# Value matmuls of two key steps side by side, and the division and the split of the maxima on GpSimd, in a four-layer cross-attention and expert network

## The chip, the cores and the metric

The kernel runs on 1 core of a Trainium2 chip (trn2). The metric is the device time of one execution in microseconds (us). Three executions of the kernel before gave 4185.41, 4183.80 and 4180.53 us, with a median of 4183.8 us. The engines are named as in the profile: PE (TensorE matmuls), PEld (TensorE weight loads), DVE (VectorE), ACT (ScalarE), POOL (GpSimd), SP (SyncE, which here only issues DMAs).

## The reference

A sequence x of 2048 tokens with 256 features goes through four layers. Each layer adds a cross-attention over a context of 1601 rows with 192 features, and then a mixture of experts. The change touches the attention alone. Cut to what matters:

```python
def xattn(x, y):                       # x: 2048 x 256 (normalized), y: 1601 x 192
    q, k, v = heads(x @ Wq + bq), heads(y @ Wk + bk), heads(y @ Wv + bv)
    att = softmax(q @ k.T / sqrt(dh))  # per head: 2048 x 1601
    return concat(att @ v) @ Wo + bo
for L in range(4):
    x = x + xattn[L](layernorm(x), ctx)    # 16 heads of 16; layer 2: 8 heads of 32
    x = x + experts[L](layernorm(x))
```

All is in 32-bit floats in the reference. The kernel computes scores from bf16 parts of queries and keys that together hold the 32-bit value, and the rest in 32-bit floats.

## The kernel before, in words

**Tiles.** The attention of a layer goes over the tokens in `NQ` = 4 iterations of 512 queries, and in each over `NG` = 4 groups of heads: 4 heads of width 16 in layers 0, 1 and 3 (called the narrow layers below), 2 heads of width 32 in layer 2. A group goes over the keys in `NK` = 13 steps of 128 keys (the last one 65). So a layer has 16 groups and 208 steps.

**One step.** PE writes transposed scores of 128 keys by 512 queries into PSUM, two results side by side as a pair (`scores`, L1909, matmul at L1920). ACT takes the exponential of a pair in one instruction into an SBUF buffer of probabilities (`exps`, L1048, instruction at L1058). A step of a narrow layer has two pairs, made of four matmuls; a step of layer 2 has one pair, also made of four matmuls, since a head there takes two. PE then multiplies the values of the step before with those probabilities (`weigh`, L1926, matmul at L1934): one 32-bit matmul per head, each of which the trace shows as two records of 512 columns, into 32 output rows of bank 4 (64 in layer 2). Heads of a group stand on different columns of the array. The last value block of a group is issued in step 0 of the next.

**Side jobs.** Before a group's exponentials the row maxima must be known. So PE also computes, for the next group or the one after, scores with queries on the partitions (`side`, L1861, matmul at L1892), 400 columns each, and DVE reduces each to a maximum straight from PSUM (`side` of the DVE block, L1312, instruction at L1323). A group needs 64 such `max` jobs (32 in layer 2), and one `turn` job: PE transposes the maxima (L1895), DVE negates them (L1330) and splits them into three bf16 parts (L1332 to L1335), and SP moves these to memory and back into row 96 and on of the queries. `side_schedule` (L69) cuts the jobs of a group into 13 slots, about five to a step in the narrow layers. In the last iteration group 2 has 40 `max` jobs in its first ten steps and group 3 has none.

**PSUM.** Banks 0 to 3 hold two score pairs, bank 4 the sums, and banks 5 to 7 the side jobs: job n goes to bank 5 + n mod 3, and PE waits on `s_sf` until DVE has finished job n - 3. PE takes everything in the order in which it is written: two `max` jobs, two score matmuls, `max`, score, `max`, score, `max`, and then the value block.

**Sums.** After a group ACT copies bank 4 to SBUF (`copy_sums`, L1063), SP moves the row sums to 32 x 64, DVE inverts them in step 4 of the next group (L1356), SP spreads the reciprocals over `recip_wide`, and DVE divides in step 7 (`divide_sums`, L1358 to L1366): one multiplication for an even group, a multiplication and an addition for an odd one. In group 0 of each later iteration four `out` jobs, one in each of steps 8 to 11, multiply the finished heads with `Wo` (PE, L1905, two matmuls of 256 columns) and add the result to x (DVE, L1350).

**Buffers.** There are four buffers of probabilities. ACT waits on `s_pv` until the values of the pair four back are done. POOL works in the first part of a layer's attention (normalizing chunks L772, splitting queries L789 to L791, adding `bo` L856) and then waits at the fence.

Of the kernel before, what the change touches and what calls it, by code (L numbers as in the profile page):

```python
# [13 lines left out]
NG = 4  # L14
# [8 lines left out]
NF = 1024  # L23
EARLY = 5
EPS = 1e-5

# [104 lines left out]
def build(nc, A, out):  # L131
# [15 lines left out]
    with ctx:  # L147
# [45 lines left out]
        with att:  # L193
            PR = [sb(f"probs{i}", [P, 2, Q], f32, att) for i in range(4)]
            OS = [sb(f"o_sum{i}", [P, Q], f32, att) for i in range(2)]
# [13 lines left out]
            QP = [sb(f"qk_part{i}", [P, 3, Q], bf16, att) for i in range(2)]  # L209
            XNC = sb("xn_chunk", [P, TPQ, D], f32, att)  # L210
            XNQ = [XNC[:]] + [PR[d][:].rearrange("p a (b n) -> p (a b) n", n=D) for d in range(1, NQ)]
        ln2 = ExitStack()
        with ln2:
            sb("skip_sums", [P, 4 * 2 * Q + 2 * Q + 2 * 64 + 16 + 2 * Q + NG // 2 * Q + Q], f32, ln2)
# [123 lines left out]
        s_sf = sem("s_sf")  # L338
        s_mx = sem("s_mx")
        s_mp = sem("s_mp")  # L340
        s_tab = sem("s_tab")
# [417 lines left out]
        def _(pool):  # L759
# [3 lines left out]
            yd, yf = [Count(q) for q in s_yd], Count(s_yf, YF_FREE)  # L763
            kc, qe, rs, wa = Count(s_kc), Count(s_qe), Count(s_rs), Count(s_wa)
            kp, qp = Count(s_kp), Count(s_qp)
            staged = Staging({"key": Count(s_kp), "query": Count(s_qp)},
# [64 lines left out]
            for L in range(4):  # L831
# [18 lines left out]
                if L < 3:  # L850
                    wa.step(16 * 7)
                    pool.wait_ge(s_wa, wa.at())
                    pool.wait_ge(s_xn, NQ * L + L + 1)
                    pool.wait_ge(s_const, n[0])
                    for t in range(NT):
                        last = pool.tensor_tensor(X[:, t, :], X[:, t, :], BO[:], ALU.add)  # L856
                    last.then_inc(s_bo, 1)
                fence(pool, fences)
                if L < 3:
# [78 lines left out]
        def _(act):  # L938
# [68 lines left out]
            for L in range(4):  # L1007
# [40 lines left out]
                def exps(k):  # L1048
                    r = key_rows(k)
                    bias = mask_col if L == 3 else None  # L1050
                    for j in range(npair):
                        b = pair[0] % 2
                        sc.step()
                        act.wait_ge(s_sc, sc.at())
                        if pv.n > 3:
                            act.wait_ge(s_pv, pv.at(3))
                        pv.step()
                        act.activation(PR[pair[0] % 4][0:r, :, :], PS[0:r, 2 * b:2 * b + 2, :], ACT.Exp,  # L1058
                                       bias=mask_col[0:r, k:k + 1] if L == 3 else zero_col[0:r, :],
                                       scale=1.0).then_inc(s_pr, 1)  # L1060
                        pair[0] += 1
# [132 lines left out]
        def _(dve):  # L1194
# [12 lines left out]
            h, sg, dn, y, yf = Count(s_h), Count(s_sg), Count(s_y, Y_FREE), Count(s_y, Y_FREE), Count(s_yf, YF_FREE)  # L1207
            sf, rx, rs_in = Count(s_sf), Count(s_rx), Count(s_dn)
            yd = [Count(q) for q in s_yd]
# [52 lines left out]
            def normalize_chunk(c):  # L1262
                normalized(c, [XNC[:, i, :] for i in range(TPQ)])

# [19 lines left out]
            for L in range(4):  # L1284
# [27 lines left out]
                def side(job, it):  # L1312
                    bank = 5 + njob[0] % 3
                    njob[0] += 1
                    sj.step()
                    if job[0] == "turn":
                        if md.n > 0:
                            dve.wait_ge(s_md, md.at())
                        md.step(16)
                    dve.wait_ge(s_sj, sj.at())  # L1320
# [7 lines left out]
                    elif job[0] == "turn":  # L1328
                        neg, rest = MN[0:units, :], MR[0:units, :]
                        dve.tensor_scalar(neg, PS[0:units, bank, 0:P], -1.0, None, ALU.mult).then_inc(s_sf, 1)  # L1330
                        dve.wait_ge(s_sf, sf.at())
                        link(dve.tensor_copy(MP[0:units, 1, :], neg))  # L1332
                        link(dve.tensor_tensor(rest, neg, MP[0:units, 1, :], ALU.subtract))
                        link(dve.tensor_copy(MP[0:units, 2, :], rest))
                        dve.tensor_tensor(MP[0:units, 3, :], rest, MP[0:units, 2, :], ALU.subtract).then_inc(s_mp, 1)  # L1335
                    elif job[0] == "den":
# [5 lines left out]
                    elif job[0] == "spread":  # L1342
                        pair = OT[:, job[1] // 2, :]
                        dve.tensor_tensor(OS[1][:], OS[1][:], PS[:, bank, :], ALU.mult).then_inc(s_sf, 1)
                        dve.wait_ge(s_sf, sf.at())
                        dve.tensor_tensor(pair, pair, OS[1][:], ALU.add).then_inc(s_ot, 1)
                    else:
                        t = (it - 1) * TPQ + job[1]
# [8 lines left out]

                def divide_sums(g):  # L1358
                    rx.step(16 * hpg)
                    dve.wait_ge(s_rx, rx.at())  # L1360
                    pair = OT[:, g // 2, :]
                    if g % 2 == 0:
                        dve.tensor_tensor(pair, OS[0][:], RDX[0][:], ALU.mult).then_inc(s_ot, 1)
                    else:
                        link(dve.tensor_tensor(OS[1][:], OS[1][:], RDX[1][:], ALU.mult))
                        dve.tensor_tensor(pair, pair, OS[1][:], ALU.add).then_inc(s_ot, 1)  # L1366

                def sides(jobs, it):
                    for job in jobs:
                        sf.step()  # L1370
                        side(job, it)

                sides(side_prologue(hpg), 0)

                def iteration(it, first, last):
                    njob[0] = 0
                    for g in range(NG):
                        for k, slot in enumerate(side_schedule(g, hpg, first, last)):
                            if not (first and g == 0):
                                if k == 4:  # L1380
                                    invert_row_sums((g - 1) % NG)
# [15 lines left out]
                njob[0] = 0  # L1397
                sides([("den", NG - 1), ("spread", NG - 1)] + [("out", i) for i in range(TPQ)], NQ)
                dve.wait_ge(s_sf, sf.at())
# [350 lines left out]
        def _(pe):  # L1750
# [77 lines left out]
            for L in range(4):  # L1828
# [6 lines left out]
                turn_chunk(5, lambda i: XNC[:, i, :])  # L1835

# [24 lines left out]
                def side(job):  # L1861
# [64 lines left out]
                def weigh(g, k):  # L1926

                    r = key_rows(k)
                    for j in range(npair):
                        use.step()  # L1930
                        pe.wait_ge(s_pr, use.at())
                        for i in range(2):
                            jj = 2 * j + i
                            last = mm(PS[pw * jj:pw * jj + pw, 4, :],  # L1934
                                      V[0:r, k, (g * hpg + jj) * pw:(g * hpg + jj) * pw + pw],
                                      PR[used[0] % 4][0:r, i, :], start=k == 0, stop=k == NK - 1,
                                      skip_group_check=True)
# [52 lines left out]
                def iteration(first, last):  # L1990
                    njob[0] = 0
                    for g in range(NG):
# [4 lines left out]
                        for k, slot in enumerate(side_schedule(g, hpg, first, last)):  # L1997
# [21 lines left out]
                njob[0] = 0  # L2019
                for job in [("den", NG - 1), ("spread", NG - 1)] + [("out", i) for i in range(TPQ)]:  # L2020
                    side(job)
# [335 lines left out]
```

## Time and profile before

| | |
|---|---|
| median of three executions | 4183.8 us (4180.53 to 4185.41) |
| profiled execution, its own time | 4188.72 us |
| its span, first to last instruction | 4187.0 us |
| PE busy | 3716.8 us (89%) |
| DVE busy | 2640.9 us (63%) |
| ACT busy | 1939.5 us (46%) |
| POOL busy | 441.9 us (11%) |
| mean granted TensorE clock | 0.931 |

Busy is the time in which an engine executes an instruction. Matmuls are pipelined: a record lasts longer than its distance from the next one, so the distance between starts is the number to use for PE. Where the timeline merges neighbouring instructions it gives the first start, the time to the last end, and xcount. A part in brackets gives the idle time before an instruction and what ended it.

### The profile page before, as it was taken

What the parts mean: (1) busy time and instruction counts of PE and PEld (TensorE: products, weight loads), DVE (VectorE), ACT (ScalarE), POOL (GpSimd) and SP (SyncE); (2) the same over time, 40 slices, a digit from 0 to 9 for tenths busy, and PEclk for the clock granted to TensorE, in tenths of its full rate; (3) what the DMA queues carried; (4) which work ended last, traced back from release to release, by engine and by line L of the source; (5) the groups of instructions that cost most, each with busy time, mean ns of one, the idle gap of its engine ahead of it and who ended that gap; (6) DMA issues with size and microseconds to landing.
All of it is one profiled execution on the core that took longest, in us unless ns stands there. A gap on an engine that the chain in (4) does not pass through costs nothing. (4 is left out here: it accounts for less than half of the span.)

```text
span 4187.0 us, 52156 instructions
## 1 busy us (share of the span) xinstructions
PE 3716.8 (89%) x17670; PEld 1632.2 (39%) x17671; DVE 2640.9 (63%) x5738; ACT 1939.5 (46%) x2350; POOL 441.9 (11%) x734
## 2 busy tenths in 40 slices
PE   5999999899899999946996699998989999995894
PEld 2333332566433333234664233334533333323562
DVE  4889886544689988632223566663468988974222
ACT  2677768222257777811332244443105777772110
POOL 4200000300210000032002500000321000002102
PEclk8999999799899999967998799998899999996997
DMA  7100000410100000053114100000400000002244
GB/s 132 40 14 18 16 14 6 83 24 20 35 25 15 18 16 14 6 191 114 33 33 91 57 21 18 17 13 23 76 32 26 18 17 14 17 6 78 77 135 113
DMA packets 143425, 179.37 MB, mean 43 GB/s; under 512 B 39574, under 2 KB 121051, under 8 KB 141168
## 3 DMA queue, kind: packets, MB, share of 16 engines
q1 hardware_dynamic: 131312, 135.80, 11.7%
q0 software_dynamic: 11904, 40.88, 4.3%
q8 instruction: 119, 1.95, 0.2%
q14 instruction: 90, 0.74, 0.1%
HBM read 122.81 MB, written 55.52 MB: 43 GB/s over the span
## 5 line engine op out<-in xcount | busy, mean ns | idle before, releaser
L1323 DVE TENSOR_REDUCE mx<-ps 128x1 f32<-128x400 f32 (+1 forms) x3584 | 1810.3, 566 | 386.8 <-PE ps L1892 383.5
L1058 ACT ACTIVATE probs<-ps,zero_col 128x1024 f32<-128x1024 f32 (+1 forms) x1040 | 1113.2, 1112 | 605.0 <-PE ps L1920 604.9
L1892 PE MATMUL ps<-k_stack,q_stack 97*128 97x400 bf16 (+1 forms) x3584 | 1096.8, 342 | 85.5 <-issue 27.1
L1920 PE MATMUL ps<-q_stack,k_stack 100*128 100x512 bf16 (+2 forms) x3328 | 1058.5, 381 | 5.4 <-ACT probs L1058 5.4
L1934 PE MATMUL ps<-probs,v 128*32 128x512 f32 (+2 forms) x5824 | 891.1, 607 | 0.2 <-ACT probs L1058 0.2
L1892 PEld LDWEIGHTS ps<-k_stack,q_stack 97*128 97x128 bf16 x3584 | 293.8, 97 | 1116.1 <-DVE mx L1323 715.3
L1058 ACT ACTIVATE probs<-ps,mask_col 128x1024 f32<-128x1024 f32 (+1 forms) x416 | 440.7, 1111 | 168.5 <-PE ps L1920 168.5
L1920 PEld LDWEIGHTS ps<-q_stack,k_stack 100*128 100x128 bf16 (+2 forms) x3328 | 324.0, 100 | 335.1 <-ACT probs L1058 63.2
L1600 DVE SCALAR_TENSOR_TENSOR x_res<-ps,comb,x_res 128x256 f32<-128x256 f32 x336 | 149.3, 483 | 174.2 <-PE ps L2112 160.8
L1934 PEld LDWEIGHTS ps<-probs,v 128*32 128x32 f32 (+2 forms) x5824 | 140.0, 111 | 253.1 <-issue 247.6
L783 POOL MEMSET wv<- 1x256 f32 x4 | 1.2, 305 | 1732.8 <-DVEq L382 1732.5
L2097 PE MATMUL ps<-xn_t,w_up_s 128*128 128x512 f32 x320 | 148.9, 598 | 11.1 <-DMA w_down_s<-in_down 10.2
L2112 PE MATMUL ps<-w_down_s,h_t_s 128*128 128x256 f32 x640 | 149.4, 381 | 4.3 <-ACT h_t_s L1148 4.1
L2176 PE MATMUL ps<-w_all,xn_t 128*128 x624 | 144.6, 385 | 3.9 <-ACT xn_t L1116 2.4
L2155 PE MATMUL ps<-w_all,xn_t 128*128 x312 | 142.7, 601 | 0.4 <-issue 0.4
L2112 PEld LDWEIGHTS ps<-w_down_s,h_t_s 128*128 128x128 f32 x640 | 120.6, 190 | 50.6 <-issue 35.7
L2176 PEld LDWEIGHTS ps<-w_all,xn_t 128*128 128x128 f32 x624 | 118.2, 192 | 43.1 <-issue 28.5
L1116 ACT ACTIVATE xn_t<-ps,tile_bias 128x128 f32<-128x128 f32 x312 | 84.9, 383 | 99.6 <-PE ps L2167 99.4
L1148 ACT ACTIVATE h_t_s<-ps 128x512 f32<-128x512 f32 x80 | 46.7, 596 | 177.0 <-PE ps L2097 176.9
L2130 PE MATMUL ps<-w_up_s,xn_t 128*128 128x512 f32 x256 | 112.8, 604 | 0.8 <-DVE x_res L1567 0.8
L1650 DVE COPY xn_t<-ps 128x512 f32<-128x512 f32 x78 | 54.0, 692 | 94.4 <-PE ps L2155 94.4
L957 ACT ACTIVATE rstd<-mv 128x16 f32<-128x16 f32 x8 | 1.7, 216 | 236.7 <-DVE mv L1235 236.7
(261 smaller groups left out, 2823.0 us busy)
## 6 DMA issues: line engine op xcount, KB each, us to landing
q_stack<-q_parts SPq DMA_DIRECT2D x384, 64.0 KB, 2.3
q_parts<-qk_part SPq DMA_DIRECT2D x32, 384.0 KB, 2.5
w_up<-in_up SPq DMA_DIRECT2D x17, 704.0 KB, 4.3
x_place<-zeros POOLq DMA_DIRECT2D x2, 5120.0 KB, 31.0
k_stack<-k_parts SPq DMA_DIRECT2D x48, 200.1 KB
k_stack<-k_parts POOLq DMA_DIRECT2D x48, 200.1 KB, 17.6
k_parts<-qk_part SPq DMA_DIRECT2D x24, 384.0 KB, 3.0
recip_wide<-row_recips SPq DMA_DIRECT2D x180, 32.0 KB, 1.8
```

Of the source, the lines that this page charges most:

```text
L1058: act.activation(PR[pair[0] % 4][0:r, :, :], PS[0:r, 2 * b:2 * b + 2, :], ACT.Exp, bias=mask_col[0:r, k:k + 1] if L == 3 else zero_col[0:r ...
L1116: last = act.activation(HB[:, q * P:(q + 1) * P], PS[:, 2 + q // 4, q % 4 * P:(q % 4 + 1) * P], ACT.Gelu, bias=BT[:, bass.ds(i, 1), q], sc ...
L1323: ins = dve.reduce_max(MX4[g % 2][:, u, c:c + 1], PS[:, bank, 0:CK[c]], AX.X)
L1600: dve.scalar_tensor_tensor(X[:, t, :], PS[:, b, 0:D], c, X[:, t, :], ALU.mult, ALU.add).then_inc(s_yf, 1)
L1892: last = mm(PS[:, bank, 0:CK[c]], QS[g][0:97, slot_of(j), qt * P:(qt + 1) * P], KS[0:97, (g * hpg + j) * nsub, CKO[c]:CKO[c] + CK[c]], sta ...
L1920: last = mm(PS[0:r, b + i, :], KS[0:rows, (g * hpg + jj) * nsub + sub, k * P:k * P + r], QS[g][0:rows, slot_of(jj) + sub, :], start=sub == ...
L1934: last = mm(PS[pw * jj:pw * jj + pw, 4, :], V[0:r, k, (g * hpg + jj) * pw:(g * hpg + jj) * pw + pw], PR[used[0] % 4][0:r, i, :], start=k = ...
L2097: last = mm(PS[0:rows, b, :], up[:, k, off + at:off + at + rows], xnT[:, k, c * Q:(c + 1) * Q], start=k == 0, stop=k == 1)
L2112: last = mm(PS[:, b, 0:D], HTF[(c - 1) % 2][0:rows, t, i * P:(i + 1) * P], WDF[par][0:rows, t, :], start=t == 0, stop=t == len(ft) - 1)
L2130: last = mm(PS[:, t % 8, :], xnT[:, k, t * P:(t + 1) * P], WUS[par][:, k * 512:(k + 1) * 512], start=k == 0, stop=k == 1)
L2155: last = mm(PS[:, half, :], XT1[par][:, k * P:(k + 1) * P], w1.rearrange("p a f -> p (a f)"), start=k == 0, stop=k == 1)
L2176: last = mm(PS[:, 4 + par, 0:D], HB[:, q * P:(q + 1) * P], w2.rearrange("p a f -> p (a f)"), start=q == 0, stop=q == NF // P - 1)
```

## The change

The division of the sums and the split of the maxima go from DVE to POOL, which does them in a loop over the 16 groups. DVE keeps the negation and tells POOL by a new semaphore `s_mn`; in the jobs ahead of the first group (`ahead`) DVE still does the split. Probabilities have `NPR` = 6 buffers in place of 4, and the chunk buffer `xn_chunk` is gone: its data stands in buffer 4. PE issues no value block in odd steps; in even steps from 2 on it issues those of the two steps before, one behind the other. The last of a group (step 12) still stands alone in step 0 of the next. Two `out` jobs become one: four matmuls into a whole bank, one DVE addition of 512 columns, in steps 8 and 10.

```diff
-        for i in range(TPQ):
-            slots[8 + i].append(("out", i))
+        for i in range(TPQ // 2):
+            slots[8 + 2 * i].append(("out", i))
...
-            PR = [sb(f"probs{i}", [P, 2, Q], f32, att) for i in range(4)]
+            PR = [sb(f"probs{i}", [P, 2, Q], f32, att) for i in range(NPR)]
...
+                def divide_sums(g):
+                    rx.step(16 * hpg)
+                    pool.wait_ge(s_rx, rx.at())
+                    pair = OT[:, g // 2, :]
+                    if g % 2 == 0:
+                        pool.tensor_tensor(pair, OS[0][:], RDX[0][:], ALU.mult).then_inc(s_ot, 1)
+                    else:
+                        link(pool.tensor_tensor(OS[1][:], OS[1][:], RDX[1][:], ALU.mult))
+                        pool.tensor_tensor(pair, pair, OS[1][:], ALU.add).then_inc(s_ot, 1)
+
+                def split_max_rows():
+                    pool.wait_ge(s_md, md.at())
+                    md.step(16)
+                    mn.step()
+                    pool.wait_ge(s_mn, mn.at())
+                    neg, rest = MN[0:4 * hpg, :], MR[0:4 * hpg, :]
+                    link(pool.tensor_copy(MP[0:4 * hpg, 1, :], neg))
+                    link(pool.tensor_tensor(rest, neg, MP[0:4 * hpg, 1, :], ALU.subtract))
+                    link(pool.tensor_copy(MP[0:4 * hpg, 2, :], rest))
+                    pool.tensor_tensor(MP[0:4 * hpg, 3, :], rest, MP[0:4 * hpg, 2, :], ALU.subtract).then_inc(s_mp, 1)
...
-                        if pv.n > 3:
-                            act.wait_ge(s_pv, pv.at(3))
+                        if pv.n >= NPR:
+                            act.wait_ge(s_pv, pv.at(NPR - 1))
...
-                        x = X[:, bass.ds(t, 1), :].rearrange("p a d -> p (a d)") if not isinstance(t, int) else X[:, t, :]
-                        dve.tensor_tensor(x, x, PS[:, bank, 0:D], ALU.add).then_inc(s_sf, 1)
+                        x = X[:, t:t + 2, :].rearrange("p a d -> p (a d)")
+                        dve.tensor_tensor(x, x, PS[:, bank, :], ALU.add).then_inc(s_sf, 1)
...
-                                if k == 7:
-                                    divide_sums((g - 1) % NG)
...
-                        i = job[1]
-                        for a in range(NG // 2):
-                            last = mm(PS[:, bank, 0:D], OT[:, a, i * P:(i + 1) * P], WO[:, a, :],
-                                      start=a == 0, stop=a == NG // 2 - 1)
+                        for h in range(2):
+                            i = 2 * job[1] + h
+                            for a in range(NG // 2):
+                                last = mm(PS[:, bank, h * D:(h + 1) * D], OT[:, a, i * P:(i + 1) * P], WO[:, a, :],
+                                          start=a == 0, stop=a == NG // 2 - 1)
...
-                            elif k > 0:
-                                if k == 1 and not (first and g == 0):
+                            elif k > 0 and k % 2 == 0:
+                                if k == 2 and not (first and g == 0):
                                     cs.step()
                                     pe.wait_ge(s_os, cs.at())
+                                weigh(g, k - 2)
                                 weigh(g, k - 1)
```

## Rows read from the trace of the kernel before

**Rows 1.** Windows: iteration, plain group, group with outs, last two groups, layer-2 iteration; then PE, PEld, DVE, ACT, POOL, clock.
```profile
1332.13:1488.12 155.99, 153.42 (x902) 51.41 (x901) 139.80 (x295) 112.36 (x108) 0.00 (x0) 1.00 0.06 16
1375.45:1412.70 37.25, 37.11 (x223) 12.29 (x222) 34.16 (x73) 28.04 (x27) 0.00 (x0) 1.00 0.07 17
1332.13:1375.45 43.32, 41.89 (x239) 14.51 (x238) 36.62 (x78) 28.14 (x27) 0.00 (x0) 1.00 0.05 15
1722.01:1756.09 34.08, 32.59 (x193) 9.22 (x191) 22.04 (x48) 27.84 (x28) 0.00 (x0) 1.00 0.03 6
1756.09:1783.60 27.51, 25.51 (x149) 4.84 (x148) 3.81 (x10) 25.25 (x26) 0.00 (x0) 1.00 0.03 7
2546.05:2676.45 130.40, 130.40 (x571) 42.81 (x568) 81.99 (x168) 60.63 (x57) 0.00 (x0) 1.00 0.06 18
```

**Rows 2.** Timeline of a narrow-layer step: start, length, engine.
```profile
1319.95 0.52 PE L1892 MATMUL ps<-k_stack,q_stack 97*128 97x400 bf16 x2
1320.34 2.50 DVE L1323 TENSOR_REDUCE mx<-ps 128x1 f32<-128x400 f32 x5 [0.27 <-PE ps L1892]
1320.94 2.12 ACT L1058 ACTIVATE probs<-ps,zero_col 128x1024 f32<-128x1024 f32 x2 [0.77 <-PE ps L1920]
1321.13 0.33 PE L1892 MATMUL ps<-k_stack,q_stack 97*128 97x400 bf16 x1
1321.30 0.38 PE L1920 MATMUL ps<-q_stack,k_stack 100*128 100x512 bf16 x1
1321.52 0.33 PE L1892 MATMUL ps<-k_stack,q_stack 97*128 97x400 bf16 x1
1321.79 1.06 PE L1934 MATMUL ps<-probs,v 128*32 128x512 f32 x8
1322.78 0.51 PE L1892 MATMUL ps<-k_stack,q_stack 97*128 97x400 bf16 x2
1323.16 2.50 DVE L1323 TENSOR_REDUCE mx<-ps 128x1 f32<-128x400 f32 x5 [0.33 <-PE ps L1892]
```

**Rows 3.** Timeline behind a division on DVE, where PE waits for a bank.
```profile
1346.91 2.01 DVE L1323 TENSOR_REDUCE mx<-ps 128x1 f32<-128x400 f32 x4
1347.54 0.34 PE L1892 MATMUL ps<-k_stack,q_stack 97*128 97x400 bf16 x1 [0.59 <-DVE mx L1323]
```

**Rows 4.** Groups by line of DVE in the iteration of the first row: count, busy us, mean ns.
```profile
L1356 DVE RECIPROCAL row_sum<-row_sum 32x64 f32<-32x64 f32 x4 | 2.1, 530 | 0.0
L1365 DVE TENSOR_TENSOR o_sum<-o_sum,recip_wide 128x512 f32<-128x512 f32 x2 | 1.4, 682 | 0.0
L1333 DVE TENSOR_TENSOR m_rest<-m_neg,m_part 16x128 f32<-16x128 f32 x4 | 1.1, 280 | 0.1
```

**Rows 5.** Timeline of two out jobs at the end of the attention.
```profile
1791.65 0.42 DVE L1350 TENSOR_TENSOR x_res<-x_res,ps 128x256 f32<-128x256 f32 x1 [0.44 <-PE ps L1905]
1792.52 0.42 DVE L1350 TENSOR_TENSOR x_res<-x_res,ps 128x256 f32<-128x256 f32 x1 [0.44 <-PE ps L1905]
```

**Rows 6.** Timeline of the last group, without side jobs, and of its end.
```profile
1764.66 4.13 ACT L1058 ACTIVATE probs<-ps,zero_col 128x1024 f32<-128x1024 f32 x4 [0.22 <-PE ps L1920]
1768.37 1.08 PE L1920 MATMUL ps<-q_stack,k_stack 100*128 100x512 bf16 x4
1769.01 2.12 ACT L1058 ACTIVATE probs<-ps,zero_col 128x1024 f32<-128x1024 f32 x2 [0.22 <-PE ps L1920]
1780.44 2.52 PE L1934 MATMUL ps<-probs,v 128*32 128x512 f32 x16
```

**Rows 7.** Timeline of layer 2: a value block and what follows it.
```profile
2504.36 1.08 PE L1934 MATMUL ps<-probs,v 128*64 128x512 f32 x4
2505.37 0.52 PE L1892 MATMUL ps<-k_stack,q_stack 97*128 97x401 bf16 x2
```

**Rows 8.** Groups by line of POOL, whole run: count, busy us, mean ns.
```profile
L789 POOL TENSOR_TENSOR qk<-qk,qk_part 128x512 f32<-128x512 f32 x45 | 52.4, 1163 | 122.3 <-ACT qk_part L981 120.4
L789 POOL TENSOR_TENSOR qk<-qk,qk_part 128x65 f32<-128x65 f32 x7 | 2.4, 337 | 0.1
```

More of the change, by code:

```diff
@@ L24 @@
 EARLY = 5
+NPR = 6
 EPS = 1e-5
@@ L209, in build @@
             QP = [sb(f"qk_part{i}", [P, 3, Q], bf16, att) for i in range(2)]
-            XNC = sb("xn_chunk", [P, TPQ, D], f32, att)
-            XNQ = [XNC[:]] + [PR[d][:].rearrange("p a (b n) -> p (a b) n", n=D) for d in range(1, NQ)]
+            XNQ = [PR[d][:].rearrange("p a (b n) -> p (a b) n", n=D) for d in (4, 1, 2, 3)]
         ln2 = ExitStack()
         with ln2:
-            sb("skip_sums", [P, 4 * 2 * Q + 2 * Q + 2 * 64 + 16 + 2 * Q + NG // 2 * Q + Q], f32, ln2)
+            sb("skip_sums", [P, NPR * 2 * Q + 2 * Q + 2 * 64 + 16 + 2 * Q + NG // 2 * Q], f32, ln2)
             sb("skip_keys", [100, 16, S], bf16, ln2)
@@ L857, in _ @@
                     last.then_inc(s_bo, 1)
+                hpg = ATT[L]["hpg"]
+                mn.step()
[11 more added lines that the diff above has]
+                    pool.wait_ge(s_md, md.at())
+                    md.step(16)
+                    mn.step()
+                    pool.wait_ge(s_mn, mn.at())
[4 more added lines that the diff above has]
+                    pool.tensor_tensor(MP[0:4 * hpg, 3, :], rest, MP[0:4 * hpg, 2, :], ALU.subtract).then_inc(s_mp, 1)
+                for it in range(NQ):
+                    for g in range(NG):
+                        if it > 0 or g > 0:
+                            divide_sums((g - 1) % NG)
+                        if it < NQ - 1 or g < NG - 1:
+                            split_max_rows()
                 fence(pool, fences)
@@ L1054, in exps @@
                         act.wait_ge(s_sc, sc.at())
-                        if pv.n > 3:
-                            act.wait_ge(s_pv, pv.at(3))
+                        if pv.n >= NPR:
+                            act.wait_ge(s_pv, pv.at(NPR - 1))
                         pv.step()
-                        act.activation(PR[pair[0] % 4][0:r, :, :], PS[0:r, 2 * b:2 * b + 2, :], ACT.Exp,
+                        act.activation(PR[pair[0] % NPR][0:r, :, :], PS[0:r, 2 * b:2 * b + 2, :], ACT.Exp,
                                        bias=mask_col[0:r, k:k + 1] if L == 3 else zero_col[0:r, :],
@@ L1262, in normalize_chunk @@
             def normalize_chunk(c):
-                normalized(c, [XNC[:, i, :] for i in range(TPQ)])
+                normalized(c, [XNQ[c][:, i, :] for i in range(TPQ)])
             def split(qk, parts, n, done):
@@ L1315, in side @@
                     sj.step()
[L1316 to L1319, printed above, removed]
                     dve.wait_ge(s_sj, sj.at())
@@ L1331, in side @@
                         dve.wait_ge(s_sf, sf.at())
[L1332 to L1335, printed above, removed]
+                        dve.sem_inc(s_mn, 1)
+                        if ahead[0]:
+                            if md.n > 0:
+                                dve.wait_ge(s_md, md.at())
+                            link(dve.tensor_copy(MP[0:units, 1, :], neg))
+                            link(dve.tensor_tensor(rest, neg, MP[0:units, 1, :], ALU.subtract))
+                            link(dve.tensor_copy(MP[0:units, 2, :], rest))
+                            dve.tensor_tensor(MP[0:units, 3, :], rest, MP[0:units, 2, :], ALU.subtract).then_inc(s_mp, 1)
+                            md.step(16 * NG * NQ)
                     elif job[0] == "den":
@@ L1347, in side @@
                     else:
-                        t = (it - 1) * TPQ + job[1]
-                        x = X[:, bass.ds(t, 1), :].rearrange("p a d -> p (a d)") if not isinstance(t, int) else X[:, t, :]
-                        dve.tensor_tensor(x, x, PS[:, bank, 0:D], ALU.add).then_inc(s_sf, 1)
+                        t = (it - 1) * TPQ + 2 * job[1]
+                        x = X[:, t:t + 2, :].rearrange("p a d -> p (a d)")
+                        dve.tensor_tensor(x, x, PS[:, bank, :], ALU.add).then_inc(s_sf, 1)
                 def invert_row_sums(g):
@@ L1356, in invert_row_sums @@
                     dve.reciprocal(sums, sums).then_inc(s_rd, 1)
[L1358 to L1366, printed above, removed]
                 def sides(jobs, it):
@@ L1371, in sides @@
                         side(job, it)
+                ahead = [True]
                 sides(side_prologue(hpg), 0)
+                ahead[0] = False
                 def iteration(it, first, last):
@@ L1378, in iteration @@
                         for k, slot in enumerate(side_schedule(g, hpg, first, last)):
-                            if not (first and g == 0):
-                                if k == 4:
-                                    invert_row_sums((g - 1) % NG)
-                                if k == 7:
-                                    divide_sums((g - 1) % NG)
+                            if k == 4 and not (first and g == 0):
+                                invert_row_sums((g - 1) % NG)
                             sides(slot, it)
@@ L1397, in _ @@
                 njob[0] = 0
-                sides([("den", NG - 1), ("spread", NG - 1)] + [("out", i) for i in range(TPQ)], NQ)
+                sides([("den", NG - 1), ("spread", NG - 1)] + [("out", i) for i in range(TPQ // 2)], NQ)
                 dve.wait_ge(s_sf, sf.at())
@@ L1935, in weigh @@
                                       V[0:r, k, (g * hpg + jj) * pw:(g * hpg + jj) * pw + pw],
-                                      PR[used[0] % 4][0:r, i, :], start=k == 0, stop=k == NK - 1,
+                                      PR[used[0] % NPR][0:r, i, :], start=k == 0, stop=k == NK - 1,
                                       skip_group_check=True)
@@ L2019, in _ @@
                 njob[0] = 0
-                for job in [("den", NG - 1), ("spread", NG - 1)] + [("out", i) for i in range(TPQ)]:
+                for job in [("den", NG - 1), ("spread", NG - 1)] + [("out", i) for i in range(TPQ // 2)]:
                     side(job)
```

7 lines of the change are left out of this document (5 added, 2 removed).

## The prediction

> **What bounds the kernel now.** I read the share of each engine first, then windows by stage, then the timeline of one step. The windows show the attention of the narrow layers as a stage that PE fills and DVE nearly fills: in one iteration of 155.99 us PE is busy 153.42 and DVE 139.80, at a granted clock of 1.00, and in layer 2 PE is busy for the whole window while DVE has 81.99 of 130.40 [rows 1]. POOL is idle in all of these.
>
> The timeline of a narrow step shows how close the two are [rows 2]. On PE a `max` matmul holds the next one back by 0.17 us (1321.13 to 1321.30), a score matmul by 0.22 (1321.30 to 1321.52). The value block starts 0.27 after the last `max`, so 0.10 late, and the next `max` follows it after 0.99. That makes 5 x 0.17 + 4 x 0.22 + 0.10 + 0.99 = 2.82; the step repeats after 2.83 (1319.95 to 1322.78). So PE sets the pace. DVE needs 2.50 for its five reductions and then idles 0.33, because nothing comes from PE while the value block runs. That idle time is the key to this change: DVE has at most three banks filled when the block begins, and three reductions of 0.50 last 1.50 us.
>
> **The join.** What does a value block cost beyond its streaming? Two `out` jobs follow each other after 0.87 us [rows 5]; each is four records of 256 columns, so a 512-column record takes 0.43. A block is eight records on four column groups, two rounds, 0.87. It costs 0.10 + 0.99 = 1.09, so about 0.23 goes to getting in and out. A joined block is four rounds: 0.10 + 0.99 + 0.86 = 1.95, against 2.18 for two. The trace has one place where two blocks stand together, at the end of the attention: 16 records in 2.52 us [rows 6]. Less the 0.17 by which a last record outlasts its slot that is 2.35, but the second block there waits for its exponentials, so I keep it only as a sign that the join may give nothing. Bounds for what a join saves: 0 and 0.36 (streaming alone); I take 0.23, because the cost sits at the block's edges.
>
> The Trainium skill, TensorEngine Tiling (Array Packing), Key Properties, says that changing the tiling mode drains the engine. The 0.23 us at the block's edges agrees. By that rule alone the change makes PE's work shorter, which is the faster rival below.
>
> **What the join does to DVE.** Call T the start of the last `max` before a block. Now the next `max` comes at T + 1.26 (1321.52 to 1322.78), and DVE starts on it 0.38 later (1322.78 to 1323.16) [rows 2]. With a joined block it is T + 1.26 + 0.86 = T + 2.12, and DVE starts at T + 2.50. The `max` matmul at T could start only when the job three before it was done; where PE waits for a bank the matmul starts 0.13 after the end of the reduction (1346.91 + 0.50 to 1347.54) [rows 3]. So at T DVE has at most 1.50 - 0.13 = 1.37 us of work, and idles at least 1.13 after each joined block.
>
> Is DVE that far behind? Between two joined blocks PE has ten `max` and eight scores, 10 x 0.17 + 8 x 0.22 = 3.46 us, where DVE needs 5.0. So yes, PE catches up and waits, in the odd steps, which have no block. The two steps then repeat in 2.50 + 7 x 0.50 + 0.13 = 6.13 us: seven reductions pass until the last `max` gets its bank. Now two steps take 5.66. PE alone would need 3.46 + 1.95 = 5.41. ACT's four exponentials take 4.25; laid into the same order they end before their banks are wanted, by some tenths.
>
> **A plain narrow group** is six such pairs of steps, step 0 with its single block, and what DVE adds in a chain that it now sets: 6 x 6.13 + 2.83 + 0.53 for the reciprocals [rows 4] + about 0.05 net for the second-level maximum and a `turn` shorter than a `max` = 40.2. Now it is 37.6: the iteration of 155.99 less its `out` group of 43.32, over three [rows 1]. So +2.6, with the moved work already gone: there are 11 such groups in a layer (4, 3, 3 and 1 by iteration), +28.6.
>
> **Groups with `out` jobs** (three per layer). A double job holds PE for 4 x 0.43 = 1.73 us right before a joined block. DVE starts on it about 1.95 after T, needs some 0.68 (the length of an addition of 512 columns [rows 4]), and the next `max` arrives at T + 1.73 + 0.10 + 1.85 + 0.38 = T + 4.05. The cycle behind such a job is 1.55 longer, and each `out` takes one more place of 0.50 in the three-bank queue: 2 x 1.55 + 2 x 0.50 = +4.1 on 40.2 = 44.3, against 43.3. Three of them: +3.
>
> **The last two groups of a layer.** Here ACT decides. Group 3 has no side jobs, and ACT repeats four exponentials in 4.35 us (1764.66 to 1769.01) [rows 6]. With joined blocks the second score pair of the even step waits until its bank has been read, 2 x 1.06 + 0.10 after the first exponential began. Then come two scores (0.43), the block (0.10 + 1.85) and 0.64 from the first score to the next exponential (1768.37 to 1769.01): 5.24. That is +0.89, six times: +5.3. In group 2, with four `max` to a step until step 9, the same chain has a `max` among the last scores (0.17) and 0.99 from the block's end to the next exponential (1319.95 to 1320.94 [rows 2]): 5.76, against 2 x 2.65 on PE with four `max`. That holds for four pairs of steps, and 5.24 against 4.35 for two: +3.6.
>
> A narrow layer: 28.6 + 3 + 3.6 + 5.3 = +40.5. Three: +121.
>
> **Layer 2** has 32 `max` jobs a group. The block costs 1.01 from its start [rows 7], DVE is busy for 63% [rows 1], and three banks cover the join: two or three reductions lie between blocks. PE keeps the pace and gains 0.23 x 6 joins x 16 groups = -22.
>
> **The moved work.** POOL has not done these here. For the division the row is its own 128x512 operation, 1163 ns, against 682 on DVE [rows 4, 8]: 1.2 or 2.4 us. The reciprocals land before step 7 and the sum is wanted by the `out` job in step 8, behind the scores of that step; the two to three us fit, and for three groups of four nobody asks so early. The four steps of the split work on 16x128: between 4 x 0.34 (its 128x65 row) and 4 x 1.16 (128x512) [rows 8], against some 1.1 on DVE (280 ns each [rows 4]). I take 2 us, by the nearer row. They start in step 9, and the result is wanted four steps later, some 11 us, less two transfers. So 0 for both; DVE's relief is in the group sum above, since that counts only what stays on DVE. Queued behind POOL's wait is only POOL's next item of the same loop, and SP's move of the maxima waits for it as it did for DVE. The buffers: a pair is weighed at most five behind, so six suffice; I cost this at 0. Moving `xn_chunk` is 0 too, since the chunk is turned long before pair 4 is written.
>
> **Sum.** 121 - 22 = +99 us. The profiled execution took 4188.7, 4.9 over the median of 4183.8; added to it 4288, added to the median **4283 us**.
>
> **Rivals.**
>
> *PE keeps the pace everywhere* (faster). If DVE kept up, a join would save 0.23 in all four layers: 0.23 x 6 x 64 = -88 us, 4096. It decides at the idle time behind a joined block in the narrow layers: below 1.13 - 0.47 = 0.66 us the pairs of steps get no longer. For it: PE is the fuller engine in every window, and DVE loses about 2 us of work a group. Against: three banks hold 1.5 us and the block with its edges takes 2.12. Only a reduction of over 0.6 us, or a fourth bank, would bridge that.
>
> *The join saves nothing* (slower still). If the second block costs 1.09 like the first, the pairs take 0.23 more in the narrow layers, 0.23 x 6 x 48 = +66, and layer 2 gains 0: 4283 + 66 + 22 = 4371. For it: the 2.52 us of the adjacent blocks [rows 6].
>
> *GpSimd comes late.* If the split took the upper end and the maxima landed after step 0, PE would wait at each of 60 groups; one us each gives 4343. Against: the slack of several us.
>
> *It cancels.* If DVE's idle after a block came out near 0.75, the narrow layers would lose 0.1 a pair of steps, which layer 2 gives back: within a few us of 4184.
>
> **Chances.** Forecast 0.75; nothing saved 0.07; GpSimd late 0.03; PE keeps the pace 0.10; cancels 0.05. About 0.2% (8 us) is what a measurement of this kernel can tell from no change. Faster 0.11, same 0.04, slower 0.85. The range: the join's bounds and 0.1 us either way in the semaphore and start times of 288 pairs of steps give some -45 and +45 around 4283, and the low end reaches a little further toward the case in which less is lost: 4230 to 4330.
>
> **What would show it.** In the narrow layers: 16 records of L1934 in about 1.9 us, a `max` matmul 2.12 after the last before the block, DVE idle about 1.1 behind each block, PEld waiting for L1323 in odd steps, pairs of steps of 6.1, plain groups of 40 us. In the last group: exponentials in fours every 5.2 us, with ACT idle about 1.0. In layer 2: iterations of 124.9 where the window showed 130.4, PE full. POOL's division near 1.2 us and waited for by nobody. The prediction is wrong if DVE's idle behind a joined block is under 0.7 us, or if the granted clock in these windows leaves 1.00.

## The result and the profile after

The changed kernel takes 4251.22 us (median of four, 4248.77 to 4252.30) against 4183.12 for the kernel before in the same comparison: ratio 1.0162, 95% interval 1.0145 to 1.018. The profiled execution took 4250.8 us over a span of 4249.0, 62.0 more than before. Forecast were 4283 us and a range of 4230 to 4330.

The windows of the changed kernel that answer to [rows 1], in the same order (iteration, plain group, group with outs, group 2 and group 3 of the last iteration, iteration of layer 2). Columns as there; the last narrow window ends at the layer's last score.

```profile
1368.82:1531.49 162.67, 156.40 (x902) 53.18 (x902) 130.65 (x271) 112.57 (x109) 13.20 (x22) 1.00 0.05 15
1412.73:1452.32 39.59, 38.06 (x223) 12.66 (x223) 32.31 (x68) 28.12 (x28) 2.66 (x5) 1.00 0.06 16
1368.82:1412.73 43.91, 42.24 (x239) 15.19 (x239) 33.69 (x70) 28.22 (x28) 3.95 (x6) 1.00 0.05 15
1775.01:1811.08 36.07, 32.47 (x193) 9.65 (x191) 19.77 (x42) 27.48 (x28) 3.94 (x6) 1.00 0.02 6
1811.08:1842.00 30.92, 24.20 (x125) 5.38 (x124) 3.10 (x9) 23.04 (x23) 1.27 (x1) 0.89 0.02 6
2594.99:2719.31 124.32, 124.32 (x571) 46.39 (x568) 70.90 (x142) 60.37 (x57) 13.19 (x22) 1.00 0.07 19
```

A narrow iteration went from 155.99 to 162.67 us although DVE does less (139.80 to 130.65), and an iteration of layer 2 from 130.40 to 124.32. From a layer's first to its last score matmul, the four layers changed from 604.4, 604.5, 506.4 and 604.7 us to 635.2, 638.1, 481.2 and 636.8. That is +96.5 in the narrow layers, -25.2 in layer 2, and leaves -9.3 for everything else, which adds up to the 62.0.

The timeline of two steps of the changed kernel, which answers to [rows 2] (start, length, engine):

```profile
1326.09 4.91 DVE L1352 TENSOR_REDUCE mx<-ps 128x1 f32<-128x400 f32 x10 [0.33 <-PE ps L1916]
1329.61 0.34 PE L1916 MATMUL ps<-k_stack,q_stack 97*128 97x400 bf16 x1
1329.89 1.92 PE L1959 MATMUL ps<-probs,v 128*32 128x512 f32 x16
1331.74 0.51 PE L1916 MATMUL ps<-k_stack,q_stack 97*128 97x400 bf16 x2
1332.12 2.50 DVE L1352 TENSOR_REDUCE mx<-ps 128x1 f32<-128x400 f32 x5 [1.12 <-PE ps L1916]
1332.73 2.12 ACT L1091 ACTIVATE probs<-ps,zero_col 128x1024 f32<-128x1024 f32 x2 [1.62 <-PE ps L1945]
```

The joined block is 16 records in 1.92 us. The next `max` starts 2.13 after the last one (1329.61 to 1331.74), and DVE stands idle for 1.12 where it stood 0.33. The two steps repeat in 6.03 us (1326.09 to 1332.12), not 5.66.

In the last group of a narrow layer, which answers to [rows 6], ACT's four exponentials now come every 5.21 us instead of 4.35:

```profile
1823.29 1.04 PE L1945 MATMUL ps<-q_stack,k_stack 100*128 100x512 bf16 x4
1823.93 4.13 ACT L1091 ACTIVATE probs<-ps,zero_col 128x1024 f32<-128x1024 f32 x4 [1.08 <-PE ps L1945]
1825.10 0.60 PE L1945 MATMUL ps<-q_stack,k_stack 100*128 100x512 bf16 x2 [0.78 <-ACT probs L1091]
1829.14 2.12 ACT L1091 ACTIVATE probs<-ps,zero_col 128x1024 f32<-128x1024 f32 x2 [1.08 <-PE ps L1945]
```

The last window of the six shows a granted TensorE clock of 0.89, where the kernel before had 1.00 [rows 1]. The last group of each narrow layer (layers 0, 1 and 3, from the copy of the sums of the group before it to the copy of its own), and its first joined block in layers 0 and 1:

```profile
729.12:761.25 32.13, 24.74 (x150) 5.96 (x150) 3.10 (x9) 25.23 (x26) 1.28 (x1) 1.00 0.02 5
1810.45:1845.16 34.71, 27.73 (x150) 6.28 (x150) 3.10 (x9) 25.35 (x27) 1.27 (x1) 0.90 0.02 5
3807.28:3840.77 33.49, 26.09 (x150) 6.16 (x150) 3.10 (x9) 25.35 (x27) 1.28 (x1) 0.95 0.02 6
732.32 1.92 PE L1959 MATMUL ps<-probs,v 128*32 128x512 f32 x16
1814.08 3.64 PE L1959 MATMUL ps<-probs,v 128*32 128x512 f32 x16
```

The same group takes 32.13, 34.71 or 33.49 us as its clock is 1.00, 0.90 or 0.95; before it took 27.53 in all three layers, at 1.00. In layer 1 the clock is 0.50, the lower of its two levels (1.2 GHz), from 1813 to 1819, and the joined block in that stretch lasts 3.64 us and not 1.92. PE had just waited for exponentials (busy for 0.23 of the microsecond from 1811). It waited in the same way in layer 0, where the clock stayed at 1.00.

### The profile page after: what moved, and what is told of

Read it like the earlier page. It is cut to its first block and busy times, and to the rows that moved or that the text cites. A ratio compares the mean times of both kernels' runs of the same rounds, so it can differ in the third digit from the quotient of the medians.

```text
span 4249.0 us, 52187 instructions
## 1 busy us (share of the span) xinstructions
PE 3719.4 (88%) x17670; PEld 1664.4 (39%) x17671; DVE 2500.2 (59%) x5378; ACT 1939.8 (46%) x2350; POOL 636.5 (15%) x1062
## 5 line engine op out<-in xcount | busy, mean ns | idle before, releaser
L1352 DVE TENSOR_REDUCE mx<-ps 128x1 f32<-128x400 f32 (+1 forms) x3584 | 1788.5, 563 | 569.2 <-PE ps L1916 559.5
L1916 PE MATMUL ps<-k_stack,q_stack 97*128 97x400 bf16 (+1 forms) x3584 | 1120.3, 342 | 135.8 <-DVE mx L1352 29.9
L1959 PE MATMUL ps<-probs,v 128*32 128x512 f32 (+2 forms) x5824 | 810.2, 602 | 0.0
L1916 PEld LDWEIGHTS ps<-k_stack,q_stack 97*128 97x128 bf16 x3584 | 317.4, 97 | 1083.6 <-DVE mx L1352 750.3
L1959 PEld LDWEIGHTS ps<-probs,v 128*32 128x32 f32 (+2 forms) x5824 | 178.5, 113 | 352.2 <-issue 250.7
L869 POOL TENSOR_TENSOR o_t<-o_sum,recip_wide 128x512 f32<-128x512 f32 x32 | 40.6, 1269 | 768.1 <-DMA recip_wide<-row_recips 768.1
L871 POOL TENSOR_TENSOR o_sum<-o_sum,recip_wide 128x512 f32<-128x512 f32 x28 | 35.6, 1273 | 669.5 <-DMA recip_wide<-row_recips 669.5
L880 POOL CAST m_part<-m_neg 16x128 bf16<-16x128 f32 (+1 forms) x60 | 16.8, 279 | 649.5 <-DVEq L1361 649.5
```

Of the source, the lines that this page charges most:

```text
L1352: ins = dve.reduce_max(MX4[g % 2][:, u, c:c + 1], PS[:, bank, 0:CK[c]], AX.X)
L1916: last = mm(PS[:, bank, 0:CK[c]], QS[g][0:97, slot_of(j), qt * P:(qt + 1) * P], KS[0:97, (g * hpg + j) * nsub, CKO[c]:CKO[c] + CK[c]], sta ...
L1959: last = mm(PS[pw * jj:pw * jj + pw, 4, :], V[0:r, k, (g * hpg + jj) * pw:(g * hpg + jj) * pw + pw], PR[used[0] % NPR][0:r, i, :], start=k ...
```

## The experiments

Each ratio below is against the kernel before, run on the same chip.

**1. No joins, the rest of the change kept** (`nojoin`).

```diff
-                            elif k > 0 and k % 2 == 0:
-                                if k == 2 and not (first and g == 0):
+                            elif k > 0:
+                                if k == 1 and not (first and g == 0):
                                     cs.step()
                                     pe.wait_ge(s_os, cs.at())
-                                weigh(g, k - 2)
                                 weigh(g, k - 1)
```

> The changed kernel with a value block in every step again; GpSimd's division and split, six buffers and the double out jobs stay. Theory A (three side banks hold 1.4 us of reductions, the joined block starves VectorE): the whole loss is the join's. Plain narrow groups go back to PE's pace, 13 x 2.83 = 36.8 us (39.6 in the changed kernel, 37.6 before), since VectorE has lost 2.1 us a group; layer 2 goes back to 130.4 an iteration. About 4165 us. Rival B (GpSimd's work, or the hand-over to it, is what costs): still slower than before, 4200 to 4230 us. Rival C (the double out jobs cost): plain groups at 36.8, but the groups with outs at 44 or more, about 4185.

Measured: 4140.86 us, ratio 0.9892 (0.9875 to 0.9908). The moved work, the six buffers and the double `out` jobs together gain 45 us; the joins cost 110 on top. PE is busy through the whole of a plain group:

```profile
1395.01:1431.73 36.72, 36.72 (x223) 12.43 (x222) 32.84 (x68) 28.04 (x27) 3.95 (x6) 1.00 0.06 17
```

The expectation had 4165. Theory A (the joined block starves VectorE) had the direction right, but the gain was larger: groups with outs also fell, from 43.32 to 40.91 us. GpSimd's work is all there and the kernel is faster than before, so it isn't the cause of the loss.

**2. Joins in layer 2 alone** (`join_l2`): the branch of run 1 for `L != 2`, the joined one for layer 2.

```diff
+                            elif k > 0 and L != 2:
+                                if k == 1 and not (first and g == 0):
+                                    cs.step()
+                                    pe.wait_ge(s_os, cs.at())
+                                weigh(g, k - 1)
                             elif k > 0 and k % 2 == 0:
```

> As the kernel without joins, but in layer 2 alone the value blocks are joined. Theory A: layer 2 keeps the 25 us that the changed kernel showed there, the narrow layers lose nothing: about 4140 us, the fastest of all. Rival B: slower than before. A rival by which the join itself saves nothing gives the time of the kernel without joins.

Measured: 4112.69 us, ratio 0.9829 (0.9813 to 0.9846), 28 us faster than without joins, and faster than both kernels. Its layer 2 takes 480.9 us from first to last score (504.9 without joins), its narrow layers 589 each, as in run 1. So 24 of the 28 us lie there.

**3. The joins alone on the kernel before** (`join_alone`): six buffers and joined blocks; division, split and four `out` jobs as before. Cut to the joins:

```diff
-                            elif k > 0:
-                                if k == 1 and not (first and g == 0):
+                            elif k > 0 and k % 2 == 0:
+                                if k == 2 and not (first and g == 0):
                                     cs.step()
                                     pe.wait_ge(s_os, cs.at())
+                                weigh(g, k - 2)
                                 weigh(g, k - 1)
```

> The kernel before with the joined blocks and the six buffers alone: division and split on VectorE, four single out jobs. Theory A: VectorE sets the pace of the narrow layers and gets back 1.1 us of split and 0.7 or 1.4 us of division a group, 2.1 in the mean: plain groups about 41.7 us, and the 42 groups with side jobs cost 88 us more than in the changed kernel: about 4335 us. Rival B (GpSimd's part costs): at or below the changed kernel's 4251 us.

Measured: 4290.79 us, ratio 1.0247 (1.023 to 1.0264). The direction is theory A's, but DVE's extra work costs 40 us, not 88: a plain group takes 40.48 or 40.60 against 39.59. The timeline shows where the division of an odd group went:

```profile
1401.25 1.92 PE L1934 MATMUL ps<-probs,v 128*32 128x512 f32 x16
1402.27 0.68 DVE L1365 TENSOR_TENSOR o_sum<-o_sum,recip_wide 128x512 f32<-128x512 f32 x1
1402.99 0.69 DVE L1366 TENSOR_TENSOR o_t<-o_t,o_sum 128x512 f32<-128x512 f32 x1
1403.60 2.49 DVE L1323 TENSOR_REDUCE mx<-ps 128x1 f32<-128x400 f32 x5
```

It stands at the head of step 7, behind the joined block of step 6, so it fills the time in which DVE would idle. Plain groups with one instruction of division take 40.48, those with two 40.60: the second costs 0.12 us in place of its 0.69. What is left is the split: from the negation to the next reduction 1.32 us pass (1454.81 to 1456.13) where the changed kernel has 0.42 (1434.87 to 1435.29). In a joined kernel the division was nearly free on DVE. In the kernel before it wasn't: there a plain group with two instructions of division takes 37.98 us, one with a single instruction 37.25 or 37.44, and in run 1, with none on DVE, they take 36.72 to 36.92.

**4. Four single `out` jobs** (`join_l2_outs4`), on the kernel of run 2.

```diff
-        for i in range(TPQ // 2):
-            slots[8 + 2 * i].append(("out", i))
+        for i in range(TPQ):
+            slots[8 + i].append(("out", i))
```

> Joined blocks in layer 2 alone, and four single out jobs in steps 8 to 11 in place of two double ones. Theory: a double out holds VectorE off for 1.7 us at once, a single one for 0.87, which its banks cover better: group with outs 0.5 to 1 us shorter, nine of them in the narrow layers: 5 to 9 us faster than with double ones. Rival C (double outs cost much): 20 us or more faster. If the outs only take PE's time, no difference.

Measured: 4118.45 us, ratio 0.9835 (0.9818 to 0.9851), against 0.9829 (0.9813 to 0.9846) for run 2: the intervals overlap, and the times alone don't settle it. The traces speak against the expectation: a group with outs takes 41.58 us with single jobs and 40.89 with double ones, and all nine of the narrow layers do so. A step with a single job takes 4.03 us (1339.55 to 1343.58), one with a double job 4.89 (1344.17 to 1349.06). Less the plain step of 2.83 and the 0.87 or 1.73 of the job itself, both leave 0.33, which is paid four times or twice. The starts of the reductions that bound these two steps, first with single jobs, then with double ones (run 2):

```profile
1339.55 2.50 DVE L1352 TENSOR_REDUCE mx<-ps 128x1 f32<-128x400 f32 x5 [0.85 <-PE ps L1915]
1343.58 2.50 DVE L1352 TENSOR_REDUCE mx<-ps 128x1 f32<-128x400 f32 x5 [0.85 <-PE ps L1915]
1344.17 2.50 DVE L1352 TENSOR_REDUCE mx<-ps 128x1 f32<-128x400 f32 x5 [0.32 <-PE ps L1916]
1349.06 2.50 DVE L1352 TENSOR_REDUCE mx<-ps 128x1 f32<-128x400 f32 x5 [0.58 <-PE ps L1916]
```

**5 and 6. Half the reductions** (`half_before`, `half_after`): DVE reduces 200 of 400 columns, in the kernel before and in the changed one. The maxima leave out half of the keys; PE and ACT do all their work.

```diff
-                        ins = dve.reduce_max(MX4[g % 2][:, u, c:c + 1], PS[:, bank, 0:CK[c]], AX.X)
+                        ins = dve.reduce_max(MX4[g % 2][:, u, c:c + 1], PS[:, bank, 0:CK[c] // 2], AX.X)
```

> The kernel before with each reduction over the first half of its 400 columns (the rest of the maxima is left out); PE and ScalarE do all their work. VectorE then keeps up everywhere: the plain narrow groups fall to PE's pace of 36.8 us, as without joins on GpSimd's help, and the jobs ahead of a layer's first group go faster too: 4090 to 4140 us. Its use is to be compared with the next run.

> The changed kernel with the same halved reductions. If VectorE's starvation is the only cost of the join, PE sets the pace and the join pays in all layers: pairs of steps 5.42 us, 50 to 60 us faster than the kernel before with halved reductions. If ScalarE is a second limit close behind (a score pair of the even step waits for the second exponential of the odd step, 2.12 + 0.08 after the first began, then 0.88 of scores and maxima, 1.85 of values and 0.99 to the next exponential), pairs take 5.92 us, not 5.66, and it is some 60 us slower than the kernel before with halved reductions.

Measured: 4120.57 us, ratio 0.9848 (0.9832 to 0.9865), and 4167.62 us, ratio 0.9956 (0.9939 to 0.9973). With VectorE out of the way the joins still cost 47 us. The changed kernel's timeline shows the second limit:

```profile
1335.84 4.13 ACT L1091 ACTIVATE probs<-ps,zero_col 128x1024 f32<-128x1024 f32 x4 [0.22 <-PE ps L1945]
1338.01 0.39 PE L1945 MATMUL ps<-q_stack,k_stack 100*128 100x512 bf16 x1 [0.23 <-ACT probs L1091]
1338.90 1.92 PE L1959 MATMUL ps<-probs,v 128*32 128x512 f32 x16
1341.14 1.92 DVE L1352 TENSOR_REDUCE mx<-ps 128x1 f32<-128x200 f32 x5 [1.76 <-PE ps L1916]
1341.74 2.12 ACT L1091 ACTIVATE probs<-ps,zero_col 128x1024 f32<-128x1024 f32 x2 [1.77 <-PE ps L1945]
```

The second pair of scores of the even step waits for ACT (1338.01), and only behind it come the block and the next exponential: 5.90 us from 1335.84 to 1341.74, where 5.92 was expected.

**7 and 8. Half the reductions and half the exponentials** (`both_before`, `both_after`). ACT writes half of each probability tile and the rest keeps old values; PE multiplies all of it. The edit of the second is:

```diff
-                        act.activation(PR[pair[0] % NPR][0:r, :, :], PS[0:r, 2 * b:2 * b + 2, :], ACT.Exp,
+                        w = Q if pair[0] < NPR else Q // 2
+                        act.activation(PR[pair[0] % NPR][0:r, :, 0:w], PS[0:r, 2 * b:2 * b + 2, 0:w], ACT.Exp,
```

> The kernel before with halved reductions and, after the first four buffers of a layer are filled, exponentials over half of each score tile (half of the probabilities stay old). VectorE and ScalarE keep up everywhere; the last group of a narrow layer goes from 27.5 us to PE's 13 x 1.97 = 25.6: 6 us below the run with halved reductions alone. Its use is to be compared with the next run.

> The changed kernel with halved reductions and halved exponentials. Neither VectorE nor ScalarE limits: PE's pace alone, with 96 joins a layer that save 0.24 us each: pairs of narrow steps 5.42 us, 85 to 95 us faster than the kernel before with the same halving. If the join itself saved nothing on PE, the two would be equal, but layer 2 speaks against that.

Measured: 4106.26 us, ratio 0.9812 (0.9795 to 0.9828), and 4038.02 us, ratio 0.9649 (0.9632 to 0.9665). Now the joins pay, 68 us, less than the 85 to 95 expected. From first to last score a narrow layer takes 571 us against 585, and layer 2 479 against 506. Two steps repeat in 5.48 us:

```profile
1335.79 1.92 PE L1960 MATMUL ps<-probs,v 128*32 128x512 f32 x16
1341.27 1.92 PE L1960 MATMUL ps<-probs,v 128*32 128x512 f32 x16
```

That is 0.18 less than the 5.66 of two steps without a join, and not the 0.25 that a join saves in layer 2. A bank still comes a little late: of the three `max` matmuls that stand together the last waits for it, 0.75 us for three where free ones, 0.17 apart, would take 0.67:

```profile
1339.21 0.75 PE L1917 MATMUL ps<-k_stack,q_stack 97*128 97x400 bf16 x3
1339.61 0.10 PEld L1917 LDWEIGHTS ps<-k_stack,q_stack 97*128 97x128 bf16 x1 [0.23 <-DVE mx L1353]
```

A plain group saves 0.97 us (36.73 to 35.76), one with outs 1.65 (41.01 to 39.36), group 2 of the last iteration 0.8, and the last group of a narrow layer, at a clock of 1.00 in both, loses 2.5 (24.53 to 27.02). These make the 14 us of a narrow layer.

**9. The inversion one step later** (`recip5`), behind the joined block of step 4.

```diff
-                            if k == 4 and not (first and g == 0):
+                            if k == 5 and not (first and g == 0):
                                 invert_row_sums((g - 1) % NG)
```

> The changed kernel with VectorE's inversion of the row sums in step 5 in place of step 4, so right behind the joined block of step 4, where VectorE idles 1.13 us. Theory A: its 0.53 us then fits into that idle time: plain groups 39.1 us in place of 39.6, 13 groups a narrow layer: some 20 us faster than the changed kernel, about 4231 us. If VectorE's work sets the pace by its sum, wherever it stands, nothing changes: 4251 us.

Measured: 4233.87 us, ratio 1.012 (1.0103 to 1.0137), 17 us below the changed kernel; a plain group takes 39.22 in place of 39.59. The inversion runs while the block does, and the idle time before the next reduction shrinks from 1.12 to 0.68:

```profile
1370.81 1.92 PE L1959 MATMUL ps<-probs,v 128*32 128x512 f32 x16
1371.83 0.53 DVE L1391 RECIPROCAL row_sum<-row_sum 32x64 f32<-32x64 f32 x1
1373.04 4.91 DVE L1352 TENSOR_REDUCE mx<-ps 128x1 f32<-128x400 f32 x10 [0.68 <-PE ps L1916]
```

**10. Two banks for side jobs in place of three** (`two_banks`).

```diff
-                    bank = 5 + njob[0] % 3
-                    fresh = njob[0] < 3
+                    bank = 5 + njob[0] % 2
+                    fresh = njob[0] < 2
...
-                        if sf.n > 2:
-                            pe.wait_ge(s_sf, sf.at(2))
+                        if sf.n > 1:
+                            pe.wait_ge(s_sf, sf.at(1))
```

> The changed kernel with two banks for side jobs in place of three (bank 7 unused). Theory A: eight reductions, not seven, pass before the last maximum of the two steps gets its bank: 2.12 + 0.38 + 8 x 0.484 + 0.13 = 6.50 us a pair in place of 6.03, a plain group 2.9 us longer, VectorE idle 1.6 behind a joined block; over 42 groups +120 us, and more in the jobs ahead of a layer: 4370 to 4400 us. If the number of banks were not what counts, 4251 us.

Measured: 4572.36 us, ratio 1.0915 (1.0895 to 1.0935). The idle time is the 1.6 of the formula, the total 170 us or more above it:

```profile
1411.32 5.24 DVE L1352 TENSOR_REDUCE mx<-ps 128x1 f32<-128x400 f32 x10 [1.55 <-PE ps L1916]
1415.87 1.92 PE L1959 MATMUL ps<-probs,v 128*32 128x512 f32 x16
1418.11 2.07 DVE L1352 TENSOR_REDUCE mx<-ps 128x1 f32<-128x400 f32 x4 [1.55 <-PE ps L1916]
```

Two steps take 6.79 us. Ten reductions now last 5.24 us, so one follows the other after (5.24 - 0.56) / 9 = 0.52, not 0.484: with two banks DVE finds the next one ready a little late. With 0.52 the formula gives 2.12 + 0.38 + 8 x 0.52 + 0.13 = 6.79. A plain group is 44.4 us long, 4.8 more than with three banks; over 42 groups some 200 us. Another 57 us lie in layer 2, where the expectation had none: from first to last score it takes 538.0 us in place of 481.2, a plain group 34.0 in place of 29.9, with PE busy for 472.5 us of the 504.0 between its first and last copy of sums. So three banks were enough for the join there and two are not. The rest, some 60 of 321 us, lies mostly ahead of the layers.

## Why the prediction was right, and what was off

**The mechanism.** The step by which DVE has at most 1.37 us of work left and so idles 1.13 us behind each joined block is met almost to the digit: 1.12 and 1.13 in the trace. Run 10 changes the bank count and the idle time follows; run 9 puts work into the idle time and gets most of it for nothing (a plain group is 0.37 us shorter, the inversion lasts 0.53); run 1 takes the joins out and the loss is gone. That DVE sets the pace of the plain narrow groups is shown.

**The pair of steps.** Forecast 6.13 us, measured 6.03. The term that was mis-sized is the reduction: I read 0.50 from five in 2.50 us, but that time includes the whole last record. Five of 0.565 that start every x us last 4x + 0.565, so x = 0.484; ten in 4.91 us say the same. Seven of them make the 0.1. A plain group came to 39.59 in place of 40.2. The forecast was +99 us, the profiled spans differ by 62.0. Of the 37 us between, about 18 are the plain groups, 4 the groups with outs, 5 group 2 of the last iteration, 3 layer 2, and 9 the time outside the attention loops, which I had put at nothing; the last groups go the other way by 1.

**The narrow layers**, +121 forecast, +96.5 measured. A plain group rose by 2.0 (from 37.6), forecast 2.6; one with outs by 0.6, forecast 1; group 2 of the last iteration by 2.0, forecast 3.6. The last group was forecast at +5.3, six times 0.89; the trace has 0.86 a pair. From the group's start to the layer's last score it rose from 24.0 to 28.35 in layer 0, so by 4.4, where the clock stayed at 1.00; in layer 1 to 30.92, by 6.9, and in layer 3 to 29.69, by 5.7. The difference goes with the clock, 0.89 and 0.94 in these two windows, for which the prediction had no term. It had named a clock that leaves 1.00 as a sign that it is wrong. By that sign it failed in the last group of two layers out of three; the cost is some 4 of the 96.5 us and doesn't touch the groups that carry the sum. That the three last groups together came out near their forecast (17.0 against 15.9) is luck: the clock added what the chain fell short of.

**Layer 2**, -22 forecast, -25.2 measured: 24 joins an iteration save 6.08 us, 0.25 each, where I had 0.23. Run 2, where nothing else changes, shows 24.0, and runs 7 and 8 show that a join saves time on PE in the narrow layers too, 0.18 a pair. The rival by which it saves nothing, with the 2.52 us of [rows 6], falls: that second block waited for its exponentials.

**The moved work.** GpSimd's division takes 1.27 us (estimate 1.16), its split 0.28 + 0.42 + 0.28 + 0.42, 1.6 with the gaps (estimate 2). Both are hidden, as run 1 shows. The timeline of the changed kernel, the first and the last step of a split:

```profile
1351.80 0.28 POOL L880 CAST m_part<-m_neg 16x128 bf16<-16x128 f32 x1 [10.98 <-DVEq L1361]
1353.00 0.42 POOL L883 TENSOR_TENSOR m_part<-m_rest,m_part 16x128 bf16<-16x128 f32 x1
```

What I didn't see is how much the relief is worth by itself: 45 us with the double outs, in the kernel without joins. A narrow layer before was at PE's pace in its steady steps but lost 0.8 us in each plain group (37.6 to 36.8 in the mean), and 2.4 in a group with outs, of which 0.7 are the double jobs (run 4).

**The rival "PE keeps the pace"** had a wrong deciding point. I let it turn on DVE's idle time alone and priced it at -88. Run 6 shows ACT's chain right behind, at 5.90 us a pair: with DVE fast enough the joins still lose. The prediction called ACT's slack some tenths of a microsecond, which is right (5.90 against 6.03), but the rival forgot it. Only with both shortened does the pair come near PE's pace, 5.48 where 5.41 was worked out, and the gain is 68 us and not 88: the 0.07 are the late bank, and the last groups lose. Nor would "a reduction of over 0.6 us" have bridged the idle time to any use, since seven of them stand in the pair and make it longer.

**Not settled:** the 9 us gained outside the attention loops, most of it between layers 1 and 2; why the clock fell in the last group of layers 1 and 3 and not in that of layer 0; why the last group at a clock of 1.00 rose by 4.4 and not by six times 0.86.

## What to carry to other kernels

Grouping work on the fullest engine lengthens the stretch in which it feeds nobody. Before grouping, multiply the number of buffers between it and the next engine by that engine's time for one, and compare it with the new stretch; here three banks held 1.4 us against 2.5, and a second consumer was only 0.1 us behind. Do it only in the stages where the consumers have slack (layer 2: 28 us gained), and put small jobs of a starved engine right behind the group, where they cost nothing.

## What the runs showed of the hardware

- A merged timeline entry of n instructions spans n - 1 distances and one whole record: ten reductions of 400 columns in 4.91 us are 0.484 apart, while one record lasts 0.565.
- Joining two value blocks saved 0.25 us in layer 2, by 6.08 us over 24 joins.
- Reductions of the same shape stood 0.484 us apart with three banks and 0.52 with two.
- GpSimd's 128x512 multiplication took 1.27 us beside VectorE's reductions from PSUM. The reductions did not slow down: the nine around one such multiplication (1423 to 1427) took 564 to 565 ns, and the mean of a plain group is 563 in the changed kernel and 565 before.
- The granted TensorE clock fell to 0.50 inside the last group of layer 1 of the changed kernel, after waits of PE for exponentials, and a joined block of 16 records took 3.64 us there and 1.92 at 1.00. The group took 32.13 us at a mean clock of 1.00, 33.49 at 0.95 and 34.71 at 0.90.
